# First experts of a two-layer decoder: every expert for every token, or sorted tiles of the chosen pairs

## The chip, the cores and the metric

The kernel runs on one core of one Trainium2 chip. The metric is the device time of one execution in microseconds (us); the profiled execution's span is the time from its first to its last instruction.

## The reference

A decoder of two layers over x of 32 batches x 128 tokens x 128 features (`x_sb`, in SBUF throughout). Each layer adds self attention, cross attention and a mixture of experts to x, each on the layer norm of x. The change concerns the first layer's mixture:

```python
shared = silu(xt @ sg_w.T) * (xt @ su_w.T) @ sd_w.T        # 128 -> 256 -> 128
probs = sigmoid(xt @ router_w.T + routing_bias)            # 8 experts
topk_p, topk_idx = top_k(probs, 2)
topk_p = topk_p / sum(topk_p)
w = zeros((T, 8)).at[arange(T)[:, None], topk_idx].add(topk_p)
g, u = einsum('th,eih->tei', xt, wg), einsum('th,eih->tei', xt, wu)
y = einsum('tei,ehi->teh', silu(g) * u, wd)
x = x + shared + einsum('te,teh->th', w, y)
```

T is 4096 tokens. The reference computes all eight experts for a token and weights six of them with zero.

## The kernel before, in words

Three stages follow one another, with the engines' programs written out for each: `head_attention` for both attentions of the first layer (64 batch steps, `NB_ALL`), then the first experts; then the second layer in the same way. Each engine runs its own list of steps and meets the others through semaphores. The functions of a `Follow` (L1316) are the mixture's program; its `..._front` parts run inside the last steps of the attention (`FRONTS`), the rest behind it, each engine's after `over`, which waits until attention has been added to `x_sb` for all 64 batches.

`experts` (L1334) works on groups of four batches (512 tokens, `NMG` = 8 groups) with features in partitions. `pe_front` transposes the normalised tokens; ACT writes `xh`, rounded to float32r, and POOL `xl`, the remainder. Logits, top 2 and the weights come in two halves of 16 batches on DVE (`route_find`, `route_mark`, `route_write`): the first half in the attention's last steps, the second between the chunks (`SECOND`). The weights go through DRAM (`cT_dram`) and come back broadcast over the partitions as `share`.

A group has 18 chunks of 128 hidden features: two of the shared expert and two of each of eight experts. Per chunk, `first_products` makes gate and up, three products each (hi x hi, hi x lo, lo x hi) of 512 columns; ACT applies Silu (L1752); POOL multiplies by `share` (L1526, `pool_rest`); DVE multiplies with up (`make_hidden`, L1661); ACT rounds it (`take_hi`, L1758); DVE takes the remainder (`take_lo`, L1680); PE adds three products to `ps_y` (`last_product`). That is nine products of 512 columns a chunk and 144 chunks. Once a group, ACT copies `ps_y` out, PE turns it back (L1857), DVE adds it to `x_sb` (L1694) and takes statistics, POOL finishes the norm (L265 to L270). PE runs the first products three chunks ahead. The middle groups run in a hardware loop with tiles addressed through registers, the others are written out.

In the attention, `sp` issues per step two DMAs with the next scores' shift rows (L574) and three with parts of Q and K (L589); the exponential scores of a batch wait for its shift rows, issued two steps earlier. POOL issues the stores of the split Q and K (L655). `qk_full` is free from about step 53 on. The weights are loaded and split in `Prepare` during attention.

## Time and profile before

| what | us |
|---|---|
| median of three runs | 1271.23 |
| lowest, highest | 1256.14, 1274.16 |
| profiled execution: its time | 1260.16 |
| its span | 1258.3 |
| PE busy in the span | 1128.3 |
| DVE, ACT, POOL busy | 979.5, 761.7, 688.5 |
| mean granted clock of PE | 0.974 of full |

Busy time is the union of an engine's instructions; PE's matmuls overlap, so one takes longer than it adds. What an engine waits for, and for how long, says more than its share. The stages have different limits, so the times are read stretch by stretch.

### The profile page before, as it was taken

Reading aid. Unit: us, or ns where it says so; the run is one execution under the profiler, and the core shown is the slowest. Engines: PE = TensorE matmul, PEld = TensorE weight load, DVE = VectorE, ACT = ScalarE, POOL = GpSimd, SP = SyncE. Lnnn points to the kernel's source line nnn. Section 1 sums busy time; section 2 is a strip of 40 time slices with the busy share of each in tenths; the row PEclk is TensorE's granted clock in tenths of the full one; section 3 lists DMA queues with packets and bytes.
Section 4 is the critical chain, followed back from the end, with each engine's and each line's share of the span. In section 5 each row is a group of like instructions: output and inputs, shape, how many; then the busy total and the mean of one; then the engine's idle time right before and its main releaser. Section 6 shows DMA issues by size and latency. Waiting matters only on the chain. (4 is left out here: it accounts for less than half of the span.)

```text
span 1258.3 us, 33045 instructions
## 1 busy us (share of the span) xinstructions
PE 1128.3 (90%) x10468; PEld 784.2 (62%) x10468; DVE 979.5 (78%) x2144; ACT 761.7 (61%) x1737; POOL 688.5 (55%) x967
## 2 busy tenths in 40 slices
PE   3799998899887899999999788897899999967997
PEld 2466656566565577777777566675455555645775
DVE  5698899888876888889888757776577777657996
ACT  1377788677775455555555367675266656645775
POOL 8667788767733455656666511115756664223554
PEclk9999999899998999999999989999799999979999
DMA  5765688566513011110110010001655463043551
GB/s 144 169 138 126 128 176 181 122 133 133 122 32 138 1 68 72 67 68 9 58 67 1 1 49 1 1 1 35 129 106 117 102 134 72 3 155 113 171 195 45
DMA packets 49493, 112.67 MB, mean 90 GB/s; under 512 B 11904, under 2 KB 31648, under 8 KB 47312
## 3 DMA queue, kind: packets, MB, share of 16 engines
q1 hardware_dynamic: 38848, 86.80, 27.6%
q0 software_dynamic: 5376, 18.88, 5.0%
q10 hardware_dynamic: 5136, 5.31, 2.2%
q8 instruction: 72, 1.18, 0.4%
q14 instruction: 61, 0.50, 0.2%
HBM read 88.09 MB, written 22.02 MB: 88 GB/s over the span
## 5 line engine op out<-in xcount | busy, mean ns | idle before, releaser
L1526 POOL TENSOR_TENSOR experts_shared_out<-experts_act_out,experts_share 128x512 f32<-128x512 f32 x136 | 186.2, 1370 | 132.3 <-ACT experts_act_out L1752 123.0
L1758 ACT CAST experts_hidden_hi<-experts_hidden 128x512 fp32r<-128x512 f32 x216 | 134.0, 621 | 117.7 <-DVE experts_hidden L1661 82.6
L1680 DVE TENSOR_TENSOR experts_hidden_lo<-experts_hidden,experts_hidden_hi 128x512 fp32r<-128x512 f32 x184 | 200.9, 1092 | 3.1 <-ACT experts_hidden_hi L1758 2.7
L734 DVE TENSOR_REDUCE heads_neg_max<-heads_ps_max 128x4 f32<-128x512 f32 x256 | 169.2, 680 | 35.1 <-PE heads_ps_max L932 32.9
L1752 ACT ACTIVATE experts_act_out<-experts_ps_gate 128x512 f32<-128x512 f32 x216 | 129.0, 597 | 69.1 <-PE experts_ps_gate L1815 68.1
L809 ACT ACTIVATE heads_E<-heads_ps_exp 128x512 f32<-128x512 f32 x256 | 150.0, 603 | 23.8 <-PE heads_ps_pv L954 18.0
L1661 DVE TENSOR_TENSOR experts_hidden<-experts_shared_out,experts_ps_up 128x512 f32<-128x512 f32 x136 | 92.1, 677 | 56.4 <-POOL experts_shared_out L1526 46.7
L734 DVE TENSOR_REDUCE cross_neg_max<-cross_ps_max 128x4 f32<-128x512 f32 x128 | 86.7, 685 | 49.0 <-PE cross_ps_max L932 48.5
L1813 PE MATMUL experts_ps_y<-experts_hidden_hi,experts_down_hi 128*128 128x512 f32 x216 | 94.2, 436 | 23.7 <-DVE experts_hidden_lo L1680 18.9
L932 PE MATMUL heads_ps_max<-QK 48*128 48x128 bf16 x1024 | 103.4, 226 | 10.4 <-DMA QK<-heads_qk_parts 5.6
L265 POOL TENSOR_TENSOR norm_var_eps<-norm_moments,norm_eps 128x2 f32<-128x2 f32 (+1 forms) x72 | 22.0, 306 | 154.1 <-DVE norm_moments L258 154.1
L936 PE MATMUL heads_ps_exp<-QK 50*128 50x128 bf16 x1024 | 103.2, 223 | 0.0
L809 ACT ACTIVATE cross_E<-cross_ps_exp 128x512 f32<-128x512 f32 x128 | 76.6, 599 | 39.0 <-PE cross_ps_exp L936 20.5
L1813 PE MATMUL experts_ps_gate<-experts_xh,experts_gate_hi 128*128 128x512 f32 (+1 forms) x216 | 89.7, 415 | 8.3 <-DVE x_sb L748 4.4
L932 PEld LDWEIGHTS heads_ps_max<-QK 48*128 48x128 bf16 x1024 | 59.1, 97 | 53.0 <-issue 19.6
L1815 PE MATMUL experts_ps_gate<-experts_xl,experts_gate_hi 128*128 128x512 f32 (+1 forms) x216 | 87.5, 405 | 0.0
L1814 PE MATMUL experts_ps_gate<-experts_xh,experts_gate_lo 128*128 128x512 f32 (+1 forms) x216 | 87.4, 405 | 0.0
L1814 PE MATMUL experts_ps_y<-experts_hidden_hi,experts_down_lo 128*128 128x512 f32 x216 | 86.1, 399 | 0.0
L1815 PE MATMUL experts_ps_y<-experts_hidden_lo,experts_down_hi 128*128 128x512 f32 x216 | 85.9, 398 | 0.0
L1531 POOL TENSOR_TENSOR experts_hidden_lo<-experts_hidden,experts_hidden_hi 128x512 fp32r<-128x512 f32 x32 | 46.9, 1466 | 69.8 <-ACT experts_hidden_hi L1758 69.8
L954 PE MATMUL heads_ps_pv<-heads_E,heads_V 128*32 128x128 f32 x2048 | 84.0, 283 | 0.0
L1672 DVE TENSOR_TENSOR experts_hidden<-experts_act_out,experts_share 128x512 f32<-128x512 f32 x64 | 67.2, 1060 | 16.1 <-issue 6.5
(236 smaller groups left out, 2952.3 us busy)
## 6 DMA issues: line engine op xcount, KB each, us to landing
experts_share<-experts_cT_dram SPq DMA_DIRECT2D x7, 2304.0 KB, 8.6
experts_share<-experts_cT_dram SPq DMA_DIRECT2D x7, 2048.0 KB, 7.3
heads_qk_parts<-heads_parts POOLq DMA_DIRECT2D x32, 384.0 KB, 4.5
QK<-heads_qk_parts SPq DMA_DIRECT2D x64, 192.0 KB
QK<-heads_qk_parts SPq DMA_DIRECT2D x64, 128.0 KB
cross_qk_parts<-cross_parts POOLq DMA_DIRECT2D x16, 384.0 KB, 4.6
QK<-cross_qk_parts SPq DMA_DIRECT2D x32, 192.0 KB
QK<-heads_qk_parts SPq DMA_DIRECT2D x64, 64.0 KB
```

The costliest lines, as they stand in the source:

```text
L734: nc.vector.tensor_reduce(neg_max[:, half, heads.start:heads.stop], ps_max[:, u % 2, :].rearrange("q (h k) -> q h k", h=HU), AX.X, ALU.max ...
L809: nc.scalar.activation(E[:, half, heads.start:heads.stop, :], ps_exp[:, u % 2, :].rearrange("k (h q) -> k h q", h=HU), ACT.Exp, scale=scal ...
L932: last_max = nc.tensor.matmul(ps_max[:, u % 2, i * S:(i + 1) * S], QK[q_of][rows, 0, h, max_of], QK[q_of][rows, 1, h, max_of], start=not m ...
L936: last_exp = nc.tensor.matmul(ps_exp[:, u % 2, i * S:(i + 1) * S], QK[e_of][rows, 1, h, exp_of], QK[e_of][rows, 0, h, exp_of], start=not m ...
L1526: nc.gpsimd.tensor_tensor(as_group(shared_out[c % 2][:]), as_group(act_out[b][:]), share[t.k % 2][:, row, :, :], ALU.mult).then_inc(weight ...
L1661: nc.vector.tensor_tensor(hidden[b][:], (shared_out[c % 2] if c in both else act_out[b])[:], ps_up[:, (t.k * n_up + up_at[c]) % UPS, :], A ...
L1680: nc.vector.tensor_tensor(hidden_lo[b][:], hidden[b][:], hidden_hi[b][:].bitcast(F32), ALU.subtract).then_inc(lo_dve, 1)
L1752: nc.scalar.activation(act_out[k % HB][:], ps_gate[:, k % GATES, :], ACT.Silu).then_inc(act_ready, 1)
L1758: nc.scalar.copy(hidden_hi[b][:], hidden[b][:]).then_inc(hi_ready, 1)
L1813: nc.tensor.matmul(out, hi, rhs_hi, start=start, stop=False, skip_group_check=True)
L1814: nc.tensor.matmul(out, lo, rhs_hi, start=False, stop=False, skip_group_check=True)
L1815: return nc.tensor.matmul(out, hi, rhs_lo, start=False, stop=stop, skip_group_check=True)
```

## The change

The first layer's mixture becomes `sparse_experts`; the second keeps `experts`. Tokens now lie in partitions, and the unit is a tile of 128 rows. Thirty-two units are the shared expert on the 32 batches in order, added to `x_sb`. Seventy-eight are routed: for each half of the batches the 4096 pairs of token and chosen expert are sorted by expert, each expert's rows padded to whole tiles, (4096 + 8 x 127) // 128 = 39 tiles.

The place of a pair is counted on PE (`count`, a triangular and an all-ones matrix against the choices) and finished on DVE (`route_place`); `route_map` gives each tile its expert. POOL scatters the normalised tokens `xn` to DRAM, one indirect DMA of 128 rows per batch and choice (64). SP loads sorted tiles back; PE transposes each (`turn_in`), ACT and DVE split it, and PE reads the expert's number into a register, by which the weights are addressed. The results are stored sorted; POOL gathers them, again one indirect DMA per batch and choice (64, eight buffers); DVE adds them to `x_sb` with their weights (`mix`), and takes the statistics. POOL no longer multiplies by `share`, and `share` and its DMAs go. The sorted buffers are cleared by two DMAs from a zeroed `qk_full`, issued by SP at step `NB_ALL - 7`. Everything is written out, with no loop. Weight tiles are laid out with gate and up side by side, and the two parts of down side by side.

Cut to its core (constants, tiles, semaphores and what only repeats `experts` are left out):

```diff
+                if t.reg is None and t.k == NB_ALL - 7 and follow.sp_clear is not None:
+                    follow.sp_clear(sp)
+                if t.reg is None and t.k == NB_ALL - 2 and follow.sp_tables is not None:
+                    follow.sp_tables(sp)
...
+                if t.reg is None and t.k == NB_ALL - 8 and follow.pool_blank is not None:
+                    follow.pool_blank(pool)
...
+    SHARED = B
+    UNITS_ALL = SHARED + 2 * PER_HALF
+    TURN_IN, LAG, TURN_H = 5, 3, 1
+    FIRST, LAST = -LAG, UNITS_ALL
+    SECOND = {"logits": 0, "squash": 1, "find0": 5, "mark0": 7, "find1": 9, "mark1": 10, "count": 11, "place": 13, "map": 15}
+    MIX_FROM, MIX_EACH = SHARED + PER_HALF + 6, 2
...
+    def pool_blank(pool):
+        nc.gpsimd.memset(blank, 0.0).then_inc(blanked, 1)
+
+    def sp_clear(sp):
+
+        sp.wait_ge(blanked, 1)
+        n = 416
+        for dram in xs_dram:
+            to = dram.rearrange("(p r) d -> p (r d)", p=S).rearrange("p (k n) -> p k n", n=n)
+            sp.dma_start(to, blank[:, 0:n].unsqueeze(1).to_broadcast([S, PER_HALF * W * D // S // n, n])).then_inc(cleared, 16)
+
+    def sp_rest(sp):
+        over(sp)
+        for u in range(SHARED - 8, UNITS_ALL + 1):
+            n = u + 8
+            if exists(n) and routed(n):
+                sp.wait_ge(scattered[half_of(n)], 16 * 2 * HALF_B)
+                need(sp, rT_made, n - SHARED - RING + 1)
+                sp.dma_start(xs[n % RING][:], rows_of(xs_dram, n)).then_inc(xs_loaded[n % RING], 16)
+            n = u - 1
+            if exists(n) and routed(n):
+                sp.wait_ge(y_out, n + 1)
+                sp.dma_start(rows_of(y_dram, n), y_sb[n % RING][:]).then_inc(y_stored[n % RING], 16)
...
+    def pool_rest(pool):
+        over(pool)
+        pool.wait_ge(cleared, 32)
+        for h in range(2):
+            pool.wait_ge(placed, h + 1)
+            pool.wait_ge(xn_ready, NMG // 2 * (h + 1))
+            for b in range(h * HALF_B, (h + 1) * HALF_B):
+                if b == 2:
+                    pool_front(pool, Turn(None, NMG - 1))
+                for choice in range(2):
+                    pool.indirect_dma_start(xs_dram[h], bass.IndirectOffsetOnAxis(index[:, choice, b:b + 1], 0), xn[b // MG][:, b % MG, :], None).then_inc(scattered[h], 16)
+        for h in range(2):
+            for p in range(RING):
+                last = max(u for u in range(SHARED, SHARED + (h + 1) * PER_HALF) if u % RING == p)
+                pool.wait_ge(y_stored[p], 16 * stored_of(last))
+            for b in range(h * HALF_B, (h + 1) * HALF_B):
+                for choice in range(2):
+                    n = 2 * b + choice
+                    need(pool, mixed, n - GATHERS + 1)
+                    pool.indirect_dma_start(gathered[n % GATHERS][:], None, y_dram[h], bass.IndirectOffsetOnAxis(index[:, choice, b:b + 1], 0)).then_inc(loaded[n % GATHERS], 16)
+            for i in range(2 * h, 2 * h + 2):
+                pool.wait_ge(moments_ready, norm.SLOTS * (i + 1))
+                norm.finish(nc, pool, norm.SLOTS * i, norm.SLOTS * i, norm.SLOTS, var_ready, i + 1, rstd_ready, None, moments, var_eps)
...
+    def dve_rest(dve):
+        over(dve)
+        route_place(dve, 0)
...
+            nc.vector.tensor_tensor(hidden[u % 3][:], act_out[u % 3][:], ps_gu[:, u % 2, F:], ALU.mult).then_inc(hidden_ready, 1)
...
+            nc.vector.tensor_tensor(hT_lo[u % 3][:], ps_hT[:, u % 2, 0:F], hT_hi[u % 3][:].bitcast(F32), ALU.subtract).then_inc(lo_ready, 1)
...
+            if routed(u):
+                need(dve, y_stored[u % RING], 16 * (stored_of(u) - 1))
+                nc.vector.tensor_copy(to, high).then_inc(half_added, 1)
+            else:
+                nc.vector.tensor_tensor(to, high, to, ALU.add).then_inc(half_added, 1)
+            dve.wait_ge(half_added, u + 1)
+            nc.vector.tensor_tensor(to, low, to, ALU.add).then_inc(y_out, 1)
+
+        def mix(b):
...
+                nc.vector.scalar_tensor_tensor(row(x_sb, b), gathered[n % GATHERS][:], weight[:, choice, b:b + 1], row(x_sb, b), ALU.mult, ALU.add).then_inc(mixed, 1)
+            dve.wait_ge(mixed, 2 * b + 2)
+            nc.vector.bn_stats(stats[:, b, :], row(x_sb, b)).then_inc(stats_taken, 1)
+            dve.wait_ge(stats_taken, b + 1)
+            nc.vector.bn_aggr(moments[:, b, :], stats[:, b, :]).then_inc(moments_ready, 1)
+
+        for u in range(FIRST, LAST + 1):
+            if exists(u - 1):
+                take_out(u - 1)
+            if exists(u + LAG):
+                make_hidden(u + LAG)
+            if exists(u + TURN_H):
+                take_lo(u + TURN_H)
+            if exists(u + TURN_IN) and routed(u + TURN_IN):
+                take_x_lo(u + TURN_IN)
+            if u == 0:
+                route_map(dve, 0)
...
+            if (u - MIX_FROM) % MIX_EACH == 0 and 0 <= u - MIX_FROM < MIX_EACH * HALF_B:
+                mix((u - MIX_FROM) // MIX_EACH)
+        for b in range(min(HALF_B, (LAST - MIX_FROM) // MIX_EACH + 1), B):
+            mix(b)
...
+        def first_products(u):
+            if routed(u):
+                n = u - SHARED
+                if n % PER_HALF == 0:
+                    pe.wait_ge(mapped, n // PER_HALF + 1)
+                expert[u] = pe.value_load(expert_of[0:1, half_of(u), n % PER_HALF:n % PER_HALF + 1], min_val=1, max_val=EXP)
+                high, low = (m[:, bass.ds(expert[u] * 4, 4), :].rearrange("d a f -> d (a f)") for m in (gate_up_hi, gate_up_lo))
+                pe.wait_ge(rl_ready, n + 1)
...
+            need(pe, hidden_ready, u - 1)
+            out = ps_gu[:, u % 2, :]
+            nc.tensor.matmul(out, x_hi, high, start=True, stop=False, skip_group_check=True)
+            nc.tensor.matmul(out, x_hi, low, start=False, stop=False, skip_group_check=True)
+            nc.tensor.matmul(out, x_lo, high, start=False, stop=True, skip_group_check=True).then_inc(first_done, 1)
...
+            for c in range(2):
+                at = bass.ds(expert[u] * 2 + c, 1) if routed(u) else slice(c, c + 1)
+                both = down[:, at].rearrange("f a p d -> f (a p d)")
+                these = slice(c * W, (c + 1) * W)
+                nc.tensor.matmul(out, hT_hi[u % 3][:, these], both, start=c == 0, stop=False, skip_group_check=True)
+                last = nc.tensor.matmul(out, hT_lo[u % 3][:, these], both, start=False, stop=c == 1, skip_group_check=True)
...
+        def turn_in(u):
+            n = u - SHARED
+            pe.wait_ge(xs_loaded[n % RING], 16 * (n // RING + 1))
+            need(pe, rl_ready, n - 1)
...
+        def count(h):
+
+            pe.wait_ge(marked, h + 1)
+            pe.wait_ge(xh_ready, NMG + h)
+            rows = many[:, h].rearrange("s b e -> s (b e)")
+            nc.tensor.matmul(ps_where[h].rearrange("s b e -> s (b e)"), before[:], rows, start=True, stop=False, skip_group_check=True)
+            for b in range(HALF_B):
+                last = nc.tensor.matmul(ps_where[h][:, b + 1:, :], ones[:], many[:, h, b, :].unsqueeze(1).to_broadcast([S, HALF_B - b, EXP]),
+                                        start=False, stop=b == HALF_B - 1, skip_group_check=True)
+            last.then_inc(counted, 1)
+
+        for u in range(FIRST, LAST + 1):
+            if exists(u + LAG):
+                first_products(u + LAG)
+            if exists(u + TURN_H):
+                turn_h(u + TURN_H)
+            if exists(u):
+                last_products(u)
+            if exists(u + TURN_IN) and routed(u + TURN_IN):
+                turn_in(u + TURN_IN)
```

## Rows read from the trace of the kernel before

**Rows 1.** The page: busy time of each engine, and PE's granted clock in 40 slices.

```profile
PE 1128.3 (90%) x10468; PEld 784.2 (62%) x10468; DVE 979.5 (78%) x2144; ACT 761.7 (61%) x1737; POOL 688.5 (55%) x967
...
PEclk9999999899998999999999989999799999979999
```

**Rows 2.** Stretches: us, busy time and count by engine, PE clock, DMA share, GB/s.

```profile
382.60:720.00 337.40, 320.36 (x1352) 244.46 (x1352) 279.67 (x396) 181.50 (x304) 192.35 (x157) 0.99 0.13 51
...
398.00:404.00 6.00, 5.96 (x23) 4.77 (x24) 2.91 (x5) 2.61 (x5) 1.28 (x1) 0.72 0.70 298
...
430.00:680.00 250.00, 247.31 (x1053) 191.03 (x1054) 210.78 (x285) 140.43 (x237) 146.97 (x118) 1.00 0.13 52
```

**Rows 3.** Who waited for whom from 430 to 680 us: total, times, longest.

```profile
POOL experts_shared_out L1526 <- ACT experts_act_out L1752: 99.2, 85, 5.2
...
PEld experts_ps_y L1813 <- DVE experts_hidden_lo L1680: 17.6, 64, 1.9
```

**Rows 4.** Timeline of PE: start, duration, instruction; at the stage's begin and in its middle.

```profile
383.31 0.63 PE L1814 MATMUL experts_ps_gate<-experts_xh,experts_gate_lo 128*128 128x512 f32 x1
...
676.26 0.40 PE L1813 MATMUL experts_ps_gate<-experts_xh,experts_gate_hi 128*128 x1
676.50 0.40 PE L1814 MATMUL experts_ps_gate<-experts_xh,experts_gate_lo 128*128 x1
...
678.38 0.39 PE L1813 MATMUL experts_ps_gate<-experts_xh,experts_gate_hi 128*128 128x512 f32 x1
```

**Rows 5.** Timeline of PE's weight loads: four for transposes, eight for logits.

```profile
398.62 1.10 PEld L1804 LDWEIGHTS experts_ps_tok<-experts_router,QK 128*128 128x128 f32 x8
...
715.89 0.42 PEld L1857 LDWEIGHTS experts_ps_tok<-ident,experts_yT 128*128 128x128 f32 x4 [1.11 <-ACT experts_yT L1779]
```

**Rows 6.** DMA: one issue on POOL (timeline), then three kinds with KB and us to landing.

```profile
206.01 0.91 POOL L655 DMA_DIRECT2D heads_qk_parts<-heads_parts  x1 [0.29 <-POOL heads_parts L651]
...
heads_qk_parts<-heads_parts POOLq DMA_DIRECT2D x32, 384.0 KB, 4.5
...
heads_wq<-in_cross_q SPq DMA_DIRECT2D x1, 64.0 KB, 1.9
...
experts_rank<-in_experts_rank SPq DMA_DIRECT2D x2, 4.0 KB, 1.7
```

**Rows 7.** Timeline of DVE: dependent pair, then chunks beside idle and beside busy POOL.

```profile
381.66 0.29 DVE L1592 TENSOR_TENSOR experts_others<-experts_probs,QK 128x128 f32<-128x128 f32 x1
381.99 0.29 DVE L1593 TENSOR_TENSOR experts_others<-experts_others,QK 128x128 f32<-128x128 f32 x1
...
674.42 0.68 DVE L1661 TENSOR_TENSOR experts_hidden<-experts_act_out,experts_ps_up 128x512 f32<-128x512 f32 x1
675.02 0.68 DVE L1680 TENSOR_TENSOR experts_hidden_lo<-experts_hidden,experts_hidden_hi 128x512 fp32r<-128x512 f32 x1
...
699.74 1.82 DVE L1680 TENSOR_TENSOR experts_hidden_lo<-experts_hidden,experts_hidden_hi 128x512 fp32r<-128x512 f32 x1
```

**Rows 8.** Timeline of DVE around the end of attention.

```profile
382.31 0.29 DVE L748 TENSOR_TENSOR x_sb<-heads_ps_out,x_sb 128x128 f32<-128x128 f32 x1
...
386.99 0.37 DVE L1608 TENSOR_TENSOR QK<-experts_probs,experts_total 128x128 f32<-128x128 f32 x1
```

**Rows 9.** Timeline: SP's DMAs of step 57, ACT's shift copies of steps 59 and 60.

```profile
343.51 1.23 SPq L589 DMA_DIRECT2D QK<-heads_qk_parts  x3
...
350.40 0.24 ACT L821 COPY heads_shiftT<-heads_ps_qk 32x128 bf16<-32x128 bf16 x1
...
354.59 0.24 ACT L821 COPY heads_shiftT<-heads_ps_qk 32x128 bf16<-32x128 bf16 x1
```

**Rows 10.** Timeline of POOL: the last step of a norm's finish for eight batches.

```profile
30.11 1.66 POOL L270 TENSOR_TENSOR norm_rstd<-load_var_eps,norm_minus_half 128x8 f32<-128x8 f32 x1
```

**Rows 11.** Timeline of the end of the first experts.

```profile
712.27 0.51 PE L1813 MATMUL experts_ps_y<-experts_hidden_hi,experts_down_hi 128*128 128x512 f32 x1 [1.15 <-DVE experts_hidden_lo L1680]
...
718.98 1.01 POOL L270 TENSOR_TENSOR norm_rstd<-norm_var_eps,norm_minus_half 128x4 f32<-128x4 f32 x1
```

More of the change, by code:

```diff
@@ L502, in head_attention @@
         staging.close()
-        follow = make_follow(ctx, normed, over)
+        follow = make_follow(ctx, normed, over, qk_full[:].rearrange("d c t -> d (c t)"))
         block = ctx.enter_context(nc.Block())
@@ L1318 @@
     sp_start: Callable
+    sp_clear: Callable
+    sp_tables: Callable
     sp: Callable
+    pool_blank: Callable
     pool_front: Callable
@@ L1912, in splits @@
             whole = [sb(staging, f"experts{layer}_whole{i}", [128, len(CHUNKS[layer]), 128]) for i in range(Prepare.LATE)]
+            if layer == 0:
+                gate_up_hi, gate_up_lo, down = made
+                n = (EXP + 1) * 2
+                first, second = slice(0, n), slice(n, 2 * n)
+                return [(whole[0], a["experts0_gate_up"][:, first], gate_up_hi[:, first], gate_up_lo[:, first]),
+                        (whole[1], a["experts0_gate_up"][:, second], gate_up_hi[:, second], gate_up_lo[:, second]),
+                        (whole[0], a["experts0_down"], down[:, :, 0, :], down[:, :, 1, :])]
             return [(whole[i % Prepare.LATE][:, 0:n], a[f"experts{layer}_{kind}"], *made[2 * i:2 * i + 2])
@@ L1920, in mixture, with follow @@
             name = f"experts{layer}"
-            def follow(stack, normed, over):
+            def follow(stack, normed, over, blank):
                 w = {c: a[f"{name}_{c}"] for c in ("router", "router_bias", "rank")}
+                if layer == 0:
+                    w["tables"] = a[f"{name}_tables"]
+                    return sparse_experts(nc, sem, name, x_sb, norm, ident, QK, w, small, made, stack, normed, over, blank)
                 return experts(nc, sem, name, x_sb, norm, ident, QK, w, small, made, layer, out, stack, normed, over)
@@ L1991, in layout @@
     rank = np.tile(np.arange(EXP, 0, -1, dtype=np.float32)[None], (S, 1))
+    counts = np.concatenate([W * np.arange(COUNTS), (W * np.tri(EXP, k=-1)).reshape(-1), W * np.arange(PER_HALF)])
+    tables = np.concatenate([np.tile(counts[None], (S, 1)), np.tri(S, k=-1).T], axis=1).astype(np.float32)
     def chunked(m):
```

315 lines of the change are left out of this document (312 added, 3 removed).

## The prediction

> **What bounds the kernel now.** I read the page first, for the engines' shares and the granted clock. PE is busy 90% of the span and its clock is at 9 or 10 tenths almost everywhere [rows 1]. The change touches only the first experts, so I cut the span at their borders. Stretches come next: the first experts run from 382.6 us, when the last attention batch has been added to `x_sb`, to 720.0 us, when the last `norm_rstd` is written: 337.4 us [rows 2]. Inside, the stretch 430 to 680 has PE busy for 247 of 250 us, at full clock and with 1053 matmuls. At nine matmuls a chunk that is 117 chunks, so 2.14 us a chunk. In that stretch PE's own waits are small (17.6 us of weight loads for `hidden_lo`) while POOL idles for 99 us until ACT hands it a chunk [rows 3]. One chunk's gate product starts 2.12 us after the last one's, and the next product of 512 columns follows after some 0.235 us, a ninth of that [rows 4]. So PE's matmul columns set the end of this stage: 144 chunks x 2.14 = 308 us, plus about 30 us of filling, routing and draining. Every expert is computed for every token: 8 x 32 tiles of 128 rows, beside 32 for the shared expert. After the change it is 78 tiles, beside the same 32. Nothing outside the stage gets less work.
>
> I therefore forecast the stage's new length, put together from units of 128 rows.
>
> **One unit on PE.** Three products of 512 columns: 3 x 0.235 = 0.70 us. Two transposes: four of 128x128 take 0.42 us of weight loads, so about 0.115 each [rows 5], 0.23. Four products of 256 columns at half of 0.235, 0.118 each; a weight load repeats no slower (eight in 1.10 us, some 0.13 each at most [rows 5]); 0.47. Sum 1.40 us for a shared unit, and 1.52 for a routed one, which has the transpose of its gathered rows too.
>
> A routed unit adds on PE a load of the expert's number from SBUF into a register. The trace has no such instruction. From below: the loops of this kernel already address tiles by registers, and 2.14 us a chunk shows no cost of that, so 0 if the load hides behind matmuls already queued. From above: a whole DMA round trip of a small tile, 1.7 us (4 KB, [rows 6]), if nothing is queued behind it. The load stands behind `turn_in` of the step before, and what PE still has queued then is some of the last products, 0.3 to 0.5 us. I take 0.5 us exposed, nearer to the lower end, since one word should need less than a DMA with its completion. So 2.0 us a routed unit; both ends (1.5 and 3.2) are kept for the range.
>
> The DMA page of the Trainium skill (DMA: Bandwidth & Descriptors, section Latency and other measured facts) gives a floor of 600 ns for a `tensor_load`. All of it exposed would make 2.1 us a unit and the sum below 8 us longer; no row here shows it.
>
> **One unit on DVE.** 128x512 is repeated every 0.60 us, a 128x128 one takes 0.29, and a dependent one follows after 0.33 [rows 7]. So 256 columns: 0.34. `make_hidden` 0.34, `take_lo` 0.34, `take_out` 0.21 and 0.33 (the second waits for the first): 1.22 us, and 1.43 with `take_x_lo`. Below PE's. ACT has two of 256 and one of 128, under 1 us. To the 32 shared units are added `route_map(0)` and the second half's routing, about 42 small dependent operations x 0.32 = 13 us. DVE: 32 x 1.22 + 13 = 52 us against PE's 45; with the handoffs between them I take 55.
>
> To each two units of the second routed half `mix` adds two multiply-adds, `bn_stats` and `bn_aggr`, in a dependent chain: 0.33 + 0.33 + 0.32 + 0.2 = 1.2 us, 0.6 a unit. DVE 2.03, PE 2.0: I take 2.1 a unit there.
>
> **Start.** Until 387 us DVE finishes `find`, `mark` and the last normalisation just as before [rows 8]; `count` replaces the write. `count(0)` on PE is 17 short matmuls, some 1.5 us, mostly beside that normalisation. `route_place(0)` is ten dependent operations, 3.2 us, and stands on DVE ahead of `make_hidden(0)`. PE has run into its wait for that: it starts in earnest 9 us after `over`. It has stood idle until then, and before the change such an idle stretch was followed by slower products (0.63 us instead of 0.40, [rows 4]): 2 us more.
>
> **The scatters** hide. POOL issues 32 for each half. Its DMA now takes 0.91 us of POOL for 384 KB [rows 6], that is 768 rows of 512 bytes; one of 128 rows at addresses read from a tile is not in the trace. From below 0.9; from above 2.3 (twice that and the index read, near the landing of a small DMA). I take 1.2. The first half's 32 run from 391 us for 38 us, beside shared units that last to about 450; the second half's run behind them, beside the routed units of the first. They begin to cost at 1.7 us each. The store of a tile (64 KB, 1.9 us to landing) and the load of a sorted tile eight units ahead are also covered.
>
> **The clear** of both sorted buffers, 5.1 MB, is put into SP's queue at step 57, behind its DMAs of 343.5 us [rows 9]. Behind it stand the shift rows for batches 60 to 63, four steps' pairs. The best stretch of the trace moves 298 GB/s [rows 2]: 17 us, so it ends at 362, while the exponential scores of batch 60 want their shift from about 354, by the step of 4.2 us between shift copies [rows 9]. Between 0 (the queues share the engines) and 12 us; I take 5. The memset of 128x512 on POOL is 0.5 to 1 us of an engine that waits.
>
> **The tail** is new. The second half's gathers may only start when its last tile is stored: 1.9 us. Then 32 gathers x 1.2 = 38 us on POOL with PE idle, the last landing 2 us, its mix 1.2, and the last `finish` of eight batches, 0.2 + 0.2 + 1.7 = 2 us [rows 10]: 46 us in all (45.1, with a little for handoffs). The same gathers of the first half lie beside the second half's tiles. The drain of before, from the last chunks' products at 712.3 to 720.0 us [rows 11], goes; it is in the 337.4 us.
>
> **Sum.** Start 382.6 + 5 (clear) + 9 + 2 = 399; shared units 55: 454; first half 39 x 2.0 = 78: 532; second half 39 x 2.1 = 82: 614; tail 46, and 1 for the last unit's way out: 661 us, against 720.0. That is 59 us less. The profiled execution took 1260.2 us, span 1258.3; the forecast is 1260.2 - 59 = 1201 us. The median of the three runs is 1271.2, and 11 us of noise lie between the two, so the measured gain may look larger.
>
> **The rivals.**
> 1. *The register load is free.* For it: loops with registered addresses at full pitch. Then a routed unit of the first half takes 1.5 us, 20 us less for 39, and one of the second half is held by DVE at 2.03, 3 us less: 1178 us; with the clear free as well, 1173.
> 2. *POOL holds DVE.* `hidden_lo`, with two SBUF inputs, takes 0.68 us when POOL rests and 1.82 beside its multiply [rows 7]. If each of the 64 multiply-adds lost 1.1 us to a gather in the same way, the first half's 32 would add 35 us to the loop; in the tail DVE needs 16 x 3.4 = 54 us instead of POOL's 38, 16 more. In all near 45 to 50: 1248 us. The SBUF page of the Trainium skill (SBUF — State Buffer, section SBUF: two separate sides) says that a DVE operation with two SBUF inputs is locked out only against a GpSimd operation that reads SBUF; the trace agrees for `hidden_lo`. Whether the building of descriptors counts as one, no run shows.
> 3. *The indirect transfers cost 2.3 us each.* The gathers' tail grows by 32 x 1.1 = 35 us, and the scatters of the first half end at 391 + 5 + 74 + 2 = 472, 18 us after the shared units; a few more for the second half: 1260 us. Against it: 768 rows in 0.91 us. No change.
> 4. *Slower: PE stands still for each expert's number.* At a full 1.7 us with nothing hidden, a unit takes 3.2 us and the two halves 251 us instead of 160: 1292 us. It decides from 1.26 us exposed a unit, where the 59 us are eaten up. For it: the load is on PE's in-order queue, with little queued ahead, 78 times. Against it: it is a single word.
> 5. The work could also not shrink: it does, since 39 tiles hold the 4096 pairs and the eight rounded ends whatever the routing is, and the code runs exactly those.
>
> **How the numbers follow.** Forecast (within some 20 us) 0.45; rival 1 0.18; rival 2 0.12; rival 3 0.14; rival 4 0.11. Faster by over 2% means under 1235 us by the profiled execution and 1246 by the median, about what a measurement of this kernel can tell from no change: the forecast, rival 1, half of rival 2 and the low side of rival 3 (0.06), 0.75. Within 2%: the other halves, 0.14. Slower by over 2%: rival 4 at its full price, 0.11. The range runs from rival 1's side (1150) to 1262, where rival 3 still lies; beyond it stands most of rival 4.
>
> **What would show it.** A stage of some 280 us from `over` to the last `norm_rstd`; some 110 units, of which a shared one repeats each 1.7 us and a routed one each 2.0 to 2.1; PE's idle time ahead of a routed unit's first product put down to issue, about 0.5 us; 64 scatters of 1.2 us beside busy PE; a stretch of some 46 us before the end of the stage with PE idle, in which gathers repeat each 1.2 us; exponential scores of batch 60 waiting some 5 us for their shift rows. Wrong it would be if a routed unit took over 2.8 us, if PE stood for sorted rows after the shared units, or if the tail passed 80 us.

## The result and the profile after

| | before | after |
|---|---|---|
| median of four runs, us | 1269.7 | 1217.8 |
| lowest to highest, us | 1256.1 to 1274.2 | 1207.8 to 1222.4 |
| profiled execution, its span, us | 1260.2, 1258.3 | 1207.8, 1206.0 |

The ratio is 0.960, 95% interval 0.953 to 0.967: faster, by 52 us, where 59 were forecast. The profiled execution after is the fastest of its four, 10 us under their median; that of before lies 9.5 us under its own, so the two can be compared.

The page after, answering to [rows 1]:

```profile
PE 1011.2 (84%) x10238; PEld 700.3 (58%) x10238; DVE 903.5 (75%) x2462; ACT 678.3 (56%) x1737; POOL 631.1 (52%) x956
...
PEclk9599999999989799999955899995999999869999
```

PE has lost 117 us of work. Stretches, as [rows 2], cut at the borders of the new stage: until `over` (391), start, shared units, first half, second half, tail, and from there on:

```profile
0.00:391.00 391.00, 325.58 (x4878) 216.32 (x4878) 312.83 (x874) 255.74 (x606) 269.57 (x474) 0.94 0.64 142
391.00:407.00 16.00, 13.25 (x62) 10.92 (x62) 10.56 (x34) 5.06 (x11) 8.03 (x10) 0.57 0.04 16
407.00:457.00 50.00, 43.62 (x266) 36.61 (x266) 44.28 (x153) 21.17 (x60) 38.02 (x40) 0.93 0.16 59
457.00:531.00 74.00, 72.01 (x422) 57.26 (x423) 61.84 (x211) 38.57 (x127) 19.17 (x20) 1.00 0.30 91
531.00:606.00 75.00, 67.10 (x371) 50.36 (x370) 69.07 (x252) 33.13 (x109) 34.03 (x38) 1.00 0.33 90
606.00:656.00 50.00, 0.53 (x4) 0.32 (x3) 19.68 (x67) 0.00 (x0) 35.15 (x39) 0.51 0.18 46
```

PE sets the pace in the first half (72 of 74 us busy), DVE comes first in the second (69 of 75), and in the tail POOL is alone. From 663 us, the second layer, whose code did not change, takes 543 us against 536.

The chain of steps, in the forecast's own order:

| step | forecast, us | after's profile, us |
|---|---|---|
| clear delays attention's end | 5 | 8.8 (382.6 to 391.4) |
| `over` to first routed product | 9 + 2 + 55 = 66 | 65.6 (391.4 to 457.05) |
| routed units, to the last `take_out` | 78 + 82 + 1 = 161 | 150.1 (to 607.2) |
| tail | 46 | 46.6 (to 653.8) |
| stage's end against 720.0 | -59 | -66.2 |
| block end, POOL's last work to next stage | (not in the sum) | 9.3 against 2.4: +6.9 |
| second layer | (not in the sum) | +7 |

So 66 us were gained, and 14 given back behind the stage. Timeline of PE at the border of two units in the first half:

```profile
480.89 0.28 PE L2362 MATMUL experts_ps_y<-experts_down,experts_hT_lo 128*128 x1
481.01 0.27 PE L2372 MATMUL experts_ps_xT<-ident,experts_xs 128*128 128x128 f32 x1
481.48 0.49 PE L2340 MATMUL experts_ps_gu<-experts_gate_up_hi,experts_rh 128*128 x1 [0.20 <-DVE experts_hidden L2178]
...
483.15 0.50 PE L2340 MATMUL experts_ps_gu<-experts_gate_up_hi,experts_rh 128*128 x1
```

The first product at 481.48 comes 1.96 us behind that of the unit before (479.52), the next one 1.67 us behind it: units alternate in about this way, 1.75 us on average. Between the transpose of `xs` and the first product stands the register load. The profile has it as work of PE's sequencer, which takes in PE's instructions and is not counted as busy; minimum, median and longest in ns:

```profile
L2330 PEldq TENSOR_LOAD <-experts_expert_of x78: 296/302/505, 455.9 to 599.2; - x78
L2330 PEldq FUSED_REGOPS  x78: 151/151/165, 456.5 to 599.6; - x78
```

So a load occupies the sequencer for 0.30 us and the working out of its address for 0.15, and part of that shows as up to 0.2 us of idle PE. DVE in the second half, a unit with a mix (`hidden` from 571.08 to 573.75):

```profile
571.08 0.41 DVE L2178 TENSOR_TENSOR experts_hidden<-experts_act_out,experts_ps_gu 128x256 f32<-128x256 f32 x1
571.41 0.42 DVE L2183 TENSOR_TENSOR experts_hT_lo<-experts_ps_hT,experts_hT_hi 128x256 fp32r<-128x256 f32 x1
571.77 0.29 DVE L2189 TENSOR_TENSOR experts_rl<-experts_ps_xT,experts_rh 128x128 fp32r<-128x128 f32 x1
571.98 0.80 DVE L2212 SCALAR_TENSOR_TENSOR x_sb<-experts_gathered,experts_weight,x_sb 128x128 f32<-128x128 f32 x2
572.81 0.29 DVE L2214 BATCH_NORM_STATS2 experts_stats<-x_sb 128x6 f32<-128x128 f32 x1
573.14 0.18 DVE L2216 BATCH_NORM_AGGREGATE experts_moments<-experts_stats 128x2 f32<-128x6 f32 x1
```

DVE has no gap in this unit; it is the bound there, though not on average over the stage. The waits from 382 to 664 us, as [rows 3]:

```profile
POOL experts_gathered L2068 <- DMA experts_y_dram<-experts_y_sb: 54.7, 2, 52.1
DVE x_sb L2212 <- DMA experts_gathered<-experts_y_dram,experts_index: 24.5, 32, 4.8
...
POOL experts_xs_dram L2059 <- issue: 19.1, 63, 0.3
PEld experts_ps_gu L2340 <- issue: 17.9, 51, 0.6
```

Nobody waits for sorted rows. The idle time put down to issue ahead of a routed unit's first product is there as forecast, but 17.9 us in all, not the 39 of 78 x 0.5. DVE waits 24.5 us for gathers, all of it in the tail: POOL sets it. The end of the block on POOL: the last gather, the last norm, the next stage's first work.

```profile
648.32 0.95 POOL L2068 DMA_INDIRECT experts_gathered<-experts_y_dram,experts_index  x1 [0.30 <-issue]
...
652.14 1.64 POOL L270 TENSOR_TENSOR norm_rstd<-experts_var_eps,norm_minus_half 128x8 f32<-128x8 f32 x1
663.04 4.02 POOL L619 MEMSET cross_V<- 128x1056 f32 x4 [9.27 <-POOLq L108]
```

And the one thing that the clear did to attention, on PE:

```profile
360.32 0.26 PE L938 MATMUL heads_ps_max<-QK 48*128 48x128 bf16 x1 [10.06 <-DMA QK<-heads_shiftT]
```

### The profile page after: what moved, and what is told of

It is laid out like the page before. It is cut to its first block and busy times, and to the rows that moved or that the text cites. A ratio compares the mean times of both kernels' runs of the same rounds, so it can differ in the third digit from the quotient of the medians.

```text
span 1206.0 us, 33476 instructions
## 1 busy us (share of the span) xinstructions
PE 1011.2 (84%) x10238; PEld 700.3 (58%) x10238; DVE 903.5 (75%) x2462; ACT 678.3 (56%) x1737; POOL 631.1 (52%) x956
## 3 DMA queue, kind: packets, MB, share of 16 engines
q8 instruction: 76, 1.25, 0.5%
## 5 line engine op out<-in xcount | busy, mean ns | idle before, releaser
L938 PE MATMUL heads_ps_max<-QK 48*128 48x128 bf16 x1024 | 102.6, 225 | 22.0 <-DMA QK<-heads_shiftT 10.1
L2068 POOL DMA_INDIRECT experts_gathered<-experts_y_dram,experts_index x64 | 61.3, 957 | 90.1 <-DMA experts_y_dram<-experts_y_sb 54.7
L2275 ACT ACTIVATE experts_act_out<-experts_ps_gu 128x256 f32<-128x256 f32 x110 | 42.4, 385 | 91.8 <-PE experts_ps_gu L2342 90.5
L2361 PE MATMUL experts_ps_y<-experts_down,experts_hT_hi 128*128 (+1 forms) x220 | 67.8, 329 | 9.6 <-DVE experts_hT_lo L2183 6.5
L2059 POOL DMA_INDIRECT experts_xs_dram<-QK,experts_index x64 | 61.6, 962 | 24.8 <-issue 19.1
L1767 ACT CAST experts_hidden_hi<-experts_hidden 128x512 fp32r<-128x512 f32 x72 | 44.7, 621 | 45.3 <-DVE experts_hidden L1681 33.7
L2178 DVE TENSOR_TENSOR experts_hidden<-experts_act_out,experts_ps_gu 128x256 f32<-128x256 f32 x110 | 45.9, 417 | 20.1 <-ACT experts_act_out L2275 15.4
L942 PEld LDWEIGHTS heads_ps_exp<-QK 50*128 50x128 bf16 x1024 | 58.1, 95 | 1.5 <-ACT heads_E L815 0.5
L1210 ACT ACTIVATE shared_E<-shared_scores,shared_neg_max 128x128 f32<-128x128 f32 x128 | 49.8, 391 | 15.4 <-DVE shared_probs L1159 15.4
L2362 PE MATMUL experts_ps_y<-experts_down,experts_hT_lo 128*128 (+1 forms) x220 | 57.9, 285 | 0.0
L960 PEld LDWEIGHTS heads_ps_pv<-heads_E,heads_V 128*32 128x32 f32 x2048 | 49.0, 110 | 13.7 <-issue 0.4
```

The lines of the kernel that those rows point to most:

```text
L938: last_max = nc.tensor.matmul(ps_max[:, u % 2, i * S:(i + 1) * S], QK[q_of][rows, 0, h, max_of], QK[q_of][rows, 1, h, max_of], start=not m ...
L942: last_exp = nc.tensor.matmul(ps_exp[:, u % 2, i * S:(i + 1) * S], QK[e_of][rows, 1, h, exp_of], QK[e_of][rows, 0, h, exp_of], start=not m ...
L960: last = nc.tensor.matmul(ps_pv[TILE * i:TILE * (i + 1), u // 2 * S:(u // 2 + 1) * S], V[p][:, j, window:window + TILE], E[:, half, h, :], ...
L1210: last = nc.scalar.activation(E[:, s, :], scores[t.k % 2][:, s // 2, s % 2, :], ACT.Exp, bias=neg_max[t.k % 2][:, s:s + 1], accum_out=sums ...
L2059: pool.indirect_dma_start(xs_dram[h], bass.IndirectOffsetOnAxis(index[:, choice, b:b + 1], 0), xn[b // MG][:, b % MG, :], None).then_inc(s ...
L2068: pool.indirect_dma_start(gathered[n % GATHERS][:], None, y_dram[h], bass.IndirectOffsetOnAxis(index[:, choice, b:b + 1], 0)).then_inc(loa ...
```

## The experiments

Twelve runs: nine changed kernels, two of them a second time, and the kernel of the result once more. Where "on top of" is not said, the edit is made to the kernel of the result. Times between steps below are from each kernel's own profile: `over` is the end of the last addition of attention's output to `x_sb`, the "shared stretch" runs from the first `hidden` to the first routed product, and a pitch is the time from one unit's first product to the next one's.

**1. The clear behind the shift rows.**

```diff
-                if t.reg is None and t.k == NB_ALL - 7 and follow.sp_clear is not None:
-                    follow.sp_clear(sp)
                 if t.reg is None and t.k == NB_ALL - 2 and follow.sp_tables is not None:
                     follow.sp_tables(sp)
+                    follow.sp_clear(sp)
```

> The two clearing transfers (5.1 MB) are issued behind the last shift rows and the tables, instead of seven steps before the end. Theory (the shift rows of batch 60 stood in one queue behind the clear): the product ps_max of that batch no longer waits 10 us, attention ends at 382 to 384 us instead of 391.4, and the whole gets 8 to 9 us shorter; the clear (15 us) ends near 395, ahead of the first scatter at 391 to 400, so at most 2 us come back there. Rival (the attention's end was late for another reason, such as fewer granted cycles): ps_max still waits and the end of attention stays at 390 or later. Second rival: the scatters, which wait for the clear, start over 5 us later against attention's end than the 8.8 us of now, and the first half waits for sorted rows: no gain.

Measured: 1196.4 us, ratio 0.939 (0.933 to 0.945). The wait is gone, `over` is at 379.7 us, scatters start 8.8 us behind it as before, and nobody waits for the clear. The theory holds for the mechanism, but the median fell by 21 us, not 9. Run a second time beside the changed kernel itself, on one chip:

> The kernel with the late clear once more, word for word, since the two kernels built on it and timed in another batch (on another chip) had PE, ACT and DVE standing for up to 12 us at a time while POOL issued scatters, and needed 121 us instead of 57 from the first hidden product to the first routed unit. Theory A (the stalls belong to the chip): on a chip that shows them at all, this kernel has them too and takes 1250 us or more; on one that doesn't, it takes 1190 to 1200 us and so does the kernel with the early load. Theory B (they belong to the two edited kernels, though these touch nothing in that stretch but the order of PE's or ACT's instructions): this kernel takes 1190 to 1200 us, and beside it on the same chip the kernel with the early load takes 1255 us or more.

> The changed kernel itself, word for word, on the same chip as the two. Theory A: its stretch from the first hidden product to the first routed unit is that of the kernel with the late clear (57 us, or some 120 if the chip shows the stalls), and its time is that kernel's plus 12 to 25 us: the wait of 10 us for the shift rows and, in most executions, the slower clock behind it (1.2 GHz for some 40 us of attention). Rival on the clock (it fell there by chance): the granted clock between 360 and 400 us is full in this profile, and the time is that of the late clear plus 9 to 12 us.

Measured: 1198.6 us, ratio 0.946 (0.939 to 0.953), against 1219.7 us, 0.964 (0.957 to 0.971): 21 us again. Stretches of 10 us, in which PE's clock is the third figure from the right; first the changed kernel:

```profile
350.00:360.00 10.00, 0.85 (x11) 0.39 (x9) 2.36 (x9) 1.43 (x3) 0.99 (x3) 0.63 1.04 363
360.00:370.00 10.00, 8.11 (x95) 5.14 (x95) 5.06 (x14) 3.85 (x9) 0.00 (x0) 0.50 0.11 35
...
390.00:400.00 10.00, 9.86 (x89) 7.33 (x81) 2.97 (x15) 4.80 (x10) 2.23 (x4) 0.50 0.01 2
```

then the one with the late clear:

```profile
350.00:360.00 10.00, 8.15 (x134) 5.31 (x129) 8.80 (x33) 7.47 (x18) 0.99 (x3) 1.00 0.03 5
360.00:370.00 10.00, 9.56 (x72) 7.28 (x73) 4.73 (x16) 5.12 (x11) 3.52 (x5) 0.53 0.86 289
...
380.00:390.00 10.00, 9.32 (x67) 8.35 (x66) 6.21 (x22) 4.70 (x9) 3.50 (x5) 0.50 0.01 2
```

In the changed kernel PE stands for the shift rows from 350 to 360 us, and behind that works at a granted clock of 0.50 (1.2 GHz) for some 40 us; in two other profiles it does so until attention's end. `over` came at 391.4, 405.4, 403.4 and 404.9 us in the four profiles with the clear at its first place, and at 374.5 to 390.5, on average 383.2, in the eight with the late one: 18 us apart. The slow stretch came in three of the four and, without the wait, in four of the eight (here from 360 us), where `over` was at 383.6 to 390.5 us; in the other four it was at 374.5 to 381.0. So the wait does not alone decide it, and whether it makes it likelier is not shown by so few profiles. Where both came, `over` lay beyond 403 us. The profiled execution of the result is the one of the four in which the clock was back at full by 370 us: the wait alone cost it 8.8 us.

**2. The clear on POOL's queue, at its first step.**

```diff
+                if t.reg is None and t.k == NB_ALL - 7 and follow.sp_clear is not None:
+                    follow.sp_clear(pool)
```

> The clear stays at its step, but is issued by POOL into POOL's own queue. Theory (order within SP's queue is what delays the shift rows): the wait of ps_max for the shift rows of batch 60 goes from 10 us to under 2, attention ends at 382 to 385 us. Rival (the sixteen DMA engines are full with 5.1 MB, whichever queue it is in): the wait stays at 6 us or more, and attention ends at 388 us or later. Either way it costs POOL 1 to 4 us of issuing, which may delay a norm by as much.

Measured: 1217.8 us (one run); the wait is 3.4 us, POOL issues for 2.0 us, and `over` comes at 398.7 us. So order in SP's queue made 6.7 of the 10.1 us. The other 3.4 fall where the DMA engines are full (share 1.01 from 350 to 360 us), as the rival has it: each theory has a part. The slow clock came all the same (0.50 from 360 to 410 us). In this one run another queue does not save the 21 us; another time did, twice.

**3. No register load.** The expert of each tile is a constant, so the result is that of other experts.

```diff
-                expert[u] = pe.value_load(expert_of[0:1, half_of(u), n % PER_HALF:n % PER_HALF + 1], min_val=1, max_val=EXP)
+                expert[u] = 1 + (n % PER_HALF) // 5
```

> The expert of each tile is a constant, so PE loads no number from SBUF and computes with other experts' weights than the routing says (this part of the computation is changed). Theory (about 0.2 us of each load is exposed on PE, and the second half is held by DVE): the first half's 39 units take 1.73 - 0.2 = 1.53 us each, 8 us less, the second half's 2.03 us stay within 0.05; in all 8 to 10 us less. Rival A (the register load costs nothing, the 0.2 us are issue of the products): both halves stay within 1 us. Rival B (PE, not DVE, holds the second half too): both halves get 8 us shorter, 16 us in all.

Measured: 1202.6 us (one run); the first half repeats each 1.50 us instead of 1.75, 9.9 us less; the second each 1.88 instead of 1.96, 3.3 us less. Timeline of PE:

```profile
491.01 0.27 PE L2372 MATMUL experts_ps_xT<-ident,experts_xs 128*128 128x128 f32 x1
491.04 0.48 PE L2340 MATMUL experts_ps_gu<-experts_gate_up_hi,experts_rh 128*128 128x512 f32 x1
...
492.54 0.48 PE L2340 MATMUL experts_ps_gu<-experts_gate_up_hi,experts_rh 128*128 128x512 f32 x1
```

A unit of PE's work is 1.50 us, as forecast (1.52), and the load adds 0.25 to it, half of what I took. In the second half a pair of units takes 1.50 + 2.52 = 4.02 us instead of 4.05: without the load PE only comes to its wait sooner, so something other than PE holds the pairs. It is the mix on DVE, by experiment 6.

**4. The load one unit ahead** (on top of the late clear).

```diff
+            if exists(u + LAG + 1) and routed(u + LAG + 1):
+                load_expert(u + LAG + 1)
             if exists(u + TURN_H):
                 turn_h(u + TURN_H)
```

> On top of the late clear, PE loads the expert's number of the next unit one unit ahead of its use, right behind the first products of the unit before. Leaving the loads out took 0.25 us from each unit of the first half (1.75 to 1.50) and 3.4 us from the second half. Theory A (the 0.25 us are the latency of the load, for which the products behind it wait): all of it hides, the first half repeats each 1.50 to 1.55 us, the routed units take 130 to 133 us instead of 143. Theory B (they are time that PE's in-order queue spends on the load and on the addresses, wherever it stands): the pitch stays at 1.70 to 1.75 us, 0 to 3 us are gained.

> The kernel with the late clear and the early register load once more. Theory A (stalls belong to the chip): the same stretch from the first hidden product to the first routed unit as in the kernel with the late clear beside it, within 5 us. In either case the first half's pitch is again 1.64 us against 1.73 to 1.75, since the load's latency hides and ps_gu's next handoff takes over: 4 us less than with the late clear alone. Theory B: 121 us in that stretch against 57.

Measured, the second time: 1189.7 us, ratio 0.942 (0.934 to 0.949), the fastest of all that compute everything; beside it the late clear alone had 1198.6 us. First half 1.65 us a unit against 1.75, second 1.94 against 1.96; from the first routed unit to the last 137.9 us against 143.2; the other 4 us between the medians are not explained by the units. Neither theory holds whole: 0.1 of the 0.25 us hides. The first units do repeat each 1.50 us, then the pitch settles at 1.65. The trace shows where the rest went. The wait put down to issue no longer stands before the first products but before the weight loads of `turn_h`, which now come right behind the register load (from 444 to 508 us):

```profile
PEld experts_ps_hT L2350 <- issue: 8.6, 34, 0.4
```

The load still takes 0.30 us there and its address 0.15. So the rest looks like the sequencer's own time, which moved with the load; no run separates it from the handoffs between the engines. The first time it measured 1265.4 us, ratio 1.002, for another reason (below).

**5. The output's high part copied by ACT** (on top of the late clear).

```diff
-                nc.vector.tensor_copy(to, high).then_inc(half_added, 1)
+            nc.scalar.copy(y_sb[u % RING][:], ps_y[u % 2][:, 0:D]).then_inc(half_added, 1)
```

> On top of the late clear, ACT instead of DVE copies the high part of a routed unit's output out of PSUM. Theory (in the second half DVE holds the units at 1.96 us, each second one at 2.35 to 2.4 because of the mix, while PE would allow 1.75): the mean pitch falls by about the 0.21 us of the copy, to 1.75 to 1.80 us, 6 to 8 us less; the first half, which PE holds, stays at 1.75. Rival (the pitch of the second half is a chain of handoffs, into which a further engine brings its own latency): the second half stays at 1.93 us or more, and the first half may get longer.

Measured: 1273.8 us, with the stalls told below. In the part of the second half without stalls a pair of units takes 1.63 + 2.40 = 4.03 us against 1.64 + 2.41 = 4.05: nothing gained, though DVE has 0.21 us less for each unit. The rival is right. Once in each pair DVE now stands in front of `take_x_lo`, for as long as the two copies took:

```profile
642.27 0.29 DVE L2188 TENSOR_TENSOR experts_rl<-experts_ps_xT,experts_rh 128x128 fp32r<-128x128 f32 x1 [0.43 <-ACT experts_rh L2284]
```

So with the copy on ACT a handoff from ACT holds the pair instead, and the same length comes out.

**6. Without the second half's gathers; without any indirect transfer; with two scatters.** Each leaves out the multiply-adds that belong to what it leaves out, so parts of the result are missing. The last two are on top of the late clear, which by itself leaves the last column at 9.27. The times with 96, 2 and 0 transfers after the change are of one run each.

```diff
-            for b in range(h * HALF_B, (h + 1) * HALF_B):
+            for b in range(h * HALF_B, (h + 1) * HALF_B) if h == 0 else ():
```

> The second half's 32 gathers and their multiply-adds are left out (the routed part is missing from batches 16 to 31); the statistics of these batches stay. Theory (the tail is 32 gathers of 1.25 us on POOL): the stage ends 10 to 14 us after the last take_out instead of 46.9, so 33 to 37 us less. Rival (the tail is held by DVE's chain per batch): less than 20 us go. On the drain of POOL at the end of the block (9.65 us now, 2.2 before the change): if it grows with the number of indirect transfers of the block, it falls by a quarter to a third of its excess, to 7.2 to 7.8 us; if it is held only by transfers issued shortly before, it falls to 2.2 to 3 us; if by neither, it stays above 9 us.

> On top of the late clear, all 128 indirect transfers and all multiply-adds of the routed part are left out (the routed units compute on the cleared rows, and nothing of them is added). From POOL's last work to the next stage's first memset 9.27 us passed in each kernel with the indirect transfers, 128 or 96 of them, against 2.42 before the change. Theory (the presence of indirect transfers in the block makes POOL's drain longer, whatever their number): 2.3 to 3 us here. Rival (something else of the block does, such as its semaphores or its DRAM tensors): 9 us or more stay. The tail: 33 to 37 us less, as with the second half's gathers left out.

> As the kernel without indirect transfers, but with two scatters (of batch 0) kept. Theory (one or two are enough): the gap from POOL's last work to the next stage's first memset is again 9.3 us. Rival (it grows with their number, up to some limit below 96): 2.4 to 3.5 us. If the gap is 9 us without any, this kernel tells nothing more.

| indirect transfers, time in us | from the last `take_out` to POOL's last work, us | DRAIN of POOL, ns | last work to next stage, us |
|---|---|---|---|
| 128 (kernel of the result), 1217.8 | 46.6 | 9653 | 9.27 |
| 96, 1180.3 | 8.6 | 9733 | 9.35 |
| 2, 1137.3 | 8.4 | 3037 | 2.65 |
| 0, 1142.2 | 8.4 | 2870 | 2.48 |
| 0 (before the change) | none | 2225 | 2.42 |

The tail is 38 us of gathers, 32 x 1.25 less the overlap, and 8.5 of DVE's statistics and POOL's norms. POOL's rows with 96 transfers and, second, with none:

```profile
625.19 1.64 POOL L270 TENSOR_TENSOR norm_rstd<-experts_var_eps,norm_minus_half 128x8 f32<-128x8 f32 x1
636.18 4.01 POOL L619 MEMSET cross_V<- 128x1056 f32 x4 [9.35 <-POOLq L108]
```

```profile
601.07 1.64 POOL L270 TENSOR_TENSOR norm_rstd<-experts_var_eps,norm_minus_half 128x8 f32<-128x8 f32 x1
605.19 3.88 POOL L618 MEMSET cross_V<- 128x1056 f32 x4 [2.48 <-POOLq L108]
```

The 7 us go when the indirect transfers go. It is not only those shortly before the drain that cost them (with 96, the last was issued 24 us ahead of it), and neither one or two nor the step from 96 to 128 matters much; where between 2 and 96 it rises stays open. With no gathers and no multiply-adds the second half repeats each 1.74 us, as the first does (1.73): it is the mix that makes it 1.96.

**7. Four shared units last, half of the first half's mixes in the tail** (on top of late clear and early load).

```diff
-    SHARED = B
+    SHARED = B - RING
...
-    GATHERS = 8
+    GATHERS = 24
...
-        for b in range(min(HALF_B, (LAST - MIX_FROM) // MIX_EACH + 1), B):
+        for b in range(MIX_IN, B):
```

> Late clear and early register load, and two more moves. The last four shared units stand behind the routed ones, where PE idles for 46 us while POOL issues the second half's gathers; and only 8 of the first half's 16 mixes stand beside the second half's units, the other 8 in the tail, where DVE has 24 us of waiting (24 gather buffers instead of 8). Theory: the first routed unit starts 4 x 1.4 = 5.6 us earlier (51 us behind the first hidden product instead of 56.4, the first half's scatters being done after 42); the second half gets 8 x 0.75 = 6 us shorter, since a pair of units with a mix takes 4.05 us and one without 3.3; the tail, which POOL's 1.25 us a gather sets, stays at 46.6 us behind the last routed take_out but for one more norm (2 us). From attention's end to the last norm 247 us instead of 256.7, the whole 9 to 10 us less than the early-load kernel: a ratio of 0.932 to 0.937 against before. Rival (DVE sets the tail once it has 24 mixes and four shared units' outputs there): the tail grows by 8 us or more and the gain is under 4 us.

Measured: 1285.0 us, ratio 1.013 (1.007 to 1.018), with the stalls, so whether it would be faster without them is not shown. What lies outside them: unmixed units of the second half repeat each 1.65 us. The tail's gathers keep 1.26 us, but from the last one to the last norm 11.8 us pass instead of 5.5, of which POOL waits 4.7 for DVE's moments: the rival's effect, 6 us, as much as the moved mixes were to save.

**The stalls.** A program is loaded onto a chip once and then timed several times. Three such loads (experiment 4 the first time, 5 and 7) spent 117 to 122 us in the shared stretch, where all the others have 56 to 58. The waits from 382 to 515 us, experiment 4:

```profile
ACT experts_act_out L2274 <- remote: 43.5, 6, 14.3
...
PEld experts_ps_y L2363 <- issue: 29.2, 5, 12.2
```

and its stretches, the first half's scatters, the second half's, and the routed units behind them:

```profile
382.00:446.00 64.00, 35.54 (x173) 28.31 (x172) 27.37 (x91) 14.83 (x38) 32.19 (x33) 0.72 0.10 38
446.00:503.00 57.00, 25.37 (x119) 20.48 (x120) 21.00 (x70) 8.56 (x27) 30.91 (x32) 0.67 0.09 37
503.00:566.00 63.00, 63.00 (x388) 49.30 (x387) 58.54 (x194) 35.31 (x116) 0.00 (x0) 1.00 0.27 77
```

PE, ACT and DVE stand for up to 16 us at a time, much of it with nothing named that they wait for, and only while POOL issues indirect transfers or within 6 us behind the last one; POOL itself keeps its 1.26 us each. When it stops, PE is busy all the time. All 26 timed runs of the three loads are long, while the kernel before, run among them, keeps its 1266 to 1270 us. It is not the program: the same kernel took 1265.4 us in one load and 1189.7 in the other. It is not the chip alone: one chip ran four kernels without stalls (experiments 1, 2, 3 and the first of 6), and the last one with them. The kernels with no scatter and with two, run on the chip of the first stalled load, had none; they have hardly an indirect transfer, so they cannot tell whether that chip stalls by itself. The traces differ in one thing more. A landing is told by sixteen updates of a semaphore, and for the first half's 32 scatters the eight profiles without stalls in which they are issued hold all 512, those of the three stalled ones 120 to 131. Whether that is a trace of the cause or a record with gaps is not shown, and what differs from load to load was not found.

## Why the forecast came out

- *What bounds the kernel.* Right: PE's columns set the stage, and 110 units instead of 144 chunks made it 66 us shorter. Since the stage lost its PE work, three engines share the bound: PE in the first half, DVE in the second, POOL in the tail.
- *One unit on PE.* Right: 1.50 us with the load left out (forecast 1.52), and 1.39 for a steady shared unit (1.40). **The term that was mis-sized is the register load**: "I take 0.5 us exposed" measured 0.25, with both ends (0 and 1.7) on their sides. It made the first half 68 us instead of 78. The Trainium skill states a floor of some 600 ns for a `tensor_load` (DMA: Bandwidth & Descriptors, section Latency and other measured facts). The profile does not agree: the 78 loads took 296 to 505 ns, 302 at the median.
- *One unit on DVE, 2.03, and 2.1 with the mix.* It measured 1.96, 5 us of the sum. That the mix on DVE holds it is shown by experiments 3 and 6; experiment 5 adds that with an operation less on DVE a wait for ACT takes its place.
- *Start and shared units, 66 us.* Measured 65.6, but with other parts: the first `hidden` 7.8 us behind `over`, then 57.9. A steady shared unit takes 1.39, but the 32 are 1.8 on average, over the 1.7 that was to show it.
- *The scatters hide.* Right; 0.96 us each and 0.3 between them, 1.25 where I took 1.2; the first half's are done 14 us before the first routed product. In the stalled loads they do not hide at all, from a cause that is no term here.
- *The clear, "between 0 and 12; I take 5".* **Mis-sized, and its second part not foreseen**: 10.1 us of waiting in the profile, 8.8 at attention's end, and 18 to 21 on average with the slow clock, which followed it in three of four profiles. I had counted a slower start after an idle PE at the stage's begin and not here, where the same idle PE stands in the middle of full work.
- *The tail, 46 us.* Measured 46.6, and by the engine named, POOL: without the second half's gathers 8.6 are left.
- *The last unit's way out, 1 us.* Too short: from the last first product to the last `take_out` 7.1 us pass, where the sum has 3.1 (a unit of 2.1 and 1).
- *What lies outside the sum.* "Nothing outside the stage gets less work" is right, but I took it for "costs the same": POOL's drain costs 7 us more. The 7 us of the second layer are no effect of the change: 543 us in this profile, and 535 to 547 in the twelve others with the same code there, the clock differing; the 536 of before lie within that. The 59 us forecast came near the 52 measured partly by luck: what was taken too long (10 us in the first half, 5 in the second) stands against what was too short or not counted (4 us of the way out, 4 of the clear, 14 behind the stage, 7 of them within the spread of the unchanged second layer). Two figures do not follow from the prediction's own terms: its sum gives a stage of 273 us, not "some 280" (262.4 were measured), and the two parts of rival 2 make 51 us.
- *Rivals.* The free register load (1) is half true. POOL holding DVE (2) is out: the 64 multiply-adds, which read two SBUF tiles, take 341 to 377 ns, also beside gathers. By the rule of the Trainium skill (SBUF — State Buffer, section SBUF: two separate sides) they would be held only by a GpSimd operation that reads SBUF. The trace does not contradict it, if issuing an indirect transfer is not one: none of the 64 took over 377 ns. Indirect transfers of 2.3 us (3) and PE at 1.7 us a load (4) are out. Rival 5 is out: the work shrank.

The rows of the gathers and multiply-adds after:

```profile
L2068 POOL DMA_INDIRECT experts_gathered<-experts_y_dram,experts_index x64: 940/944/1035, 534.3 to 648.3; - x64
L2212 DVE SCALAR_TENSOR_TENSOR x_sb<-experts_gathered,experts_weight,x_sb x64: 341/351/377, 543.5 to 650.8; 128x128 f32<-128x128 f32 x64
```

## What to carry to other kernels

Computing only what is chosen pays when the sorting and gathering lie beside work of another engine; count the part that cannot (here the last half's gathers, 32 x 1.25 us on POOL), since it takes back over a third of what the smaller work gives (38 us against the 66 that are left). A large transfer whose result is wanted much later belongs behind the small urgent ones: the same 5 MB five steps later gave 21 us for two moved lines. And look at PE's granted clock behind every gap that a change opens in full work: here a stretch at 1.2 GHz followed it in three of four profiles, and in these `over` came 12 to 14 us later than in the fourth. That the gap caused it is not shown.

## What the runs showed that I had not expected

- An indirect transfer of 128 rows occupies POOL for 0.94 to 0.96 us and is repeated each 1.25, landing 2.2 us (scatter) or 2.6 us (gather) after its issue; a plain one of 768 rows took 0.91 [rows 6]. The price is per instruction more than per row.
- A block with 96 or 128 indirect transfers ends with 9.7 us of DRAIN on POOL, one with two or none with 2.9 to 3.0.
- PE's wait of 10 us at 350 us was followed in three of four profiles by 40 us or more at 1.2 GHz; without the wait, four of eight profiles had a stretch of 28 to 42 us at 1.2 GHz that began from 360 to 370 us.
- A register load on PE takes 0.30 us of its sequencer, its address 0.15; 0.25 of it shows in a unit, and 0.15 when the load stands one unit ahead.
- In some loads of a program, and then in all runs of it, PE, ACT and DVE stand for up to 16 us at a time while POOL issues indirect transfers: 60 to 65 us in the shared stretch alone, more than the whole change gains. A kernel built on many indirect transfers should be timed in more than one load.
